# Ranks of tokens within an image pair: a scan over tiles on VectorE and three small products in place of eighteen wide ones

## Chip, cores and metric

The kernel runs on one core of one Trainium2 chip. The metric is the device time of one execution in microseconds. Three runs of the kernel before gave 541.8 us in the median (541.31 to 543.06).

PE is TensorE's matmul stream, PEld its weight loads, DVE is VectorE, ACT ScalarE, POOL GpSimd, SP SyncE.

## The reference, cut to what matters

```
x = x + conv_block(_ln_c(x))          # 16 images, 64 channels, 32x32; two binarized convolutions
t = _to_tokens(x)                     # 16384 tokens of 64
logits = _ln_t(t) @ gate_w + gate_b   # 16 experts
top_probs, top_idx = top_k(softmax(logits), 2)
hidden = silu(x @ w1[e]) * (x @ w2[e])
out = t + sum over the two chosen e of weight_e * (hidden @ w3[e])
```

Each token goes through two experts of sixteen, and gets their outputs with weights that sum to one.

## The kernel before, in words

**Routing by lines.** The sixteen experts are points of a 4 x 4 plane, and twenty lines of four points each cover every pair of points. A token is sent to the line that holds its two experts. Tokens of one line are gathered in pages of 128 tokens in DRAM, and a page is later multiplied with the four experts of its line. So each token needs a slot: the first row of its line's current page, plus its rank among the tokens of that line.

**Rounds.** The sixteen images are handled as eight pairs (q = 0 to 7). A pair is 2048 tokens: 128 partitions times TILES = 16 tiles. Each engine runs its own instruction list, written out by hand, in rounds t; in one round it works on up to five pairs at different stages: a = t (first normalization), s = t - 1 (the convolutions), b = t - 2 (second normalization, gate), r = t - 3 (choice of experts and line), z = t - 4 (slots, on DVE only). The order within a round is the order of the calls in the loops at L884 (PE), L650 (ACT) and L1520 (DVE). Semaphores join the engines.

**The steps around the change, for pair r or z.** PE's `count` (L865) gives for each token and line how many of the token's experts lie on the line. DVE's `find_line` (L1342) compares this with 1.5 and writes `line_hot`, a 0/1 array of 128 x 16 x 20. `find_line` is called between `newton_slack(0, a)` (L1246) and `newton_sum(0, a)` (L1252), two small steps of the reciprocal root `rstd` for pair a; for `rstd` wait ACT's `wide` (L576), then PE's `norm` (L831). PE's `rank` (L871 to L875) adds up in the PSUM tile `lines`: a product of `line_hot` with the strictly upper triangle (tokens of the same tile on partitions before), `left_b` (tokens left over from the pairs before, L872), and sixteen products with ones, one for each shift s in tiles, of (17 - s) x 20 columns, which add the tokens of all earlier tiles; tile 16 of the result is the total of each line. `rank` is the last call of PE's round; the first of the next is `variance(1, b)` (L819), which waits for ACT's `square2` (L602), and then the first convolution (L803). DVE's `slots(z)` (L1374 to L1414) turns ranks and totals into row numbers: twelve small steps over 20 lines, then four over 16 x 20, a reduction over lines, and a cast. Behind it stand `second_choice` (L1312 and on) with the three steps of the second root, whose second releases PE's `gate` (L848). POOL scatters the tokens of the pair to their slots (L498).

**The tail of the routing.** After pair 4 `order_pages` (L1431 to L1465) on DVE works out in which order pages are processed, PE turns it (L940), `order_rows` (L1470) casts it. SyncE waits for that before it loads pages (L392, L393). The roster of each page's experts (L1485 to L1507) and `rows_low` (L1513) stand on DVE ahead of `slots(7)`; the first expert products on PE (L971, L973) wait for both.

**The expert part**, from about 230 us of the profile on, handles 147 pages with PE, ACT and DVE in a pipeline, and scatters the results (L519). Nothing in it is touched.

## Time and profile before

| | us |
|---|---|
| median of 3 runs | 541.8 |
| lowest and highest run | 541.31, 543.06 |
| span of the profiled execution | 598.9 |
| busy in the profile: PE, PEld | 500.9, 436.7 |
| busy in the profile: DVE, ACT, POOL | 441.6, 396.0, 287.9 |

The profiled execution is longer than the runs that are timed. The page gives busy times and the chain of waits that ended last; a row of the timeline gives an instruction's start and length, and in brackets how long its engine sat idle before it and what ended that. "remote" in brackets, or "another core or an unknown queue" in the chain, is a wait whose end the profile ties to no instruction of this core. "x12" is twelve instructions merged in one row. Lengths of neighbouring rows may overlap, since the engines start an instruction before the one ahead has left.

### The profile page before, as it was taken

What the parts mean: (1) busy time and instruction counts of PE and PEld (TensorE: products, weight loads), DVE (VectorE), ACT (ScalarE), POOL (GpSimd) and SP (SyncE); (2) the same over time, 40 slices, a digit from 0 to 9 for tenths busy, and PEclk for the clock granted to TensorE, in tenths of its full rate; (3) what the DMA queues carried; (4) which work ended last, traced back from release to release, by engine and by line L of the source; (5) the groups of instructions that cost most, each with busy time, mean ns of one, the idle gap of its engine ahead of it and who ended that gap; (6) DMA issues with size and microseconds to landing.
All of it is one profiled execution on the core that took longest, in us unless ns stands there. A gap on an engine that the chain in (4) does not pass through costs nothing.

```text
span 598.9 us, 14226 instructions
## 1 busy us (share of the span) xinstructions
PE 500.9 (84%) x4186; PEld 436.7 (73%) x4186; DVE 441.6 (74%) x1242; ACT 396.0 (66%) x946; POOL 287.9 (48%) x378
## 2 busy tenths in 40 slices
PE   6899997896986627767889899999999999999854
PEld 5566665674764516757878799999998999899753
DVE  4567786685689697556676688888888888888653
ACT  5577885684765303456676588888787878778650
POOL 4000036666667675645555455454444544545351
PEclk9878997996979557879999899999999999999986
DMA  7941101011000012320122221232242425210404
GB/s 295 283 84 36 35 12 61 25 60 62 25 24 29 22 46 66 69 63 21 39 56 57 54 43 39 51 90 54 48 116 49 118 55 147 55 31 17 134 24 141
DMA packets 62664, 40.97 MB, mean 68 GB/s; under 512 B 50003, under 2 KB 54318, under 8 KB 62080
## 3 DMA queue, kind: packets, MB, share of 16 engines
q1 hardware_dynamic: 52208, 23.84, 17.5%
q0 software_dynamic: 8800, 8.94, 4.4%
q10 hardware_dynamic: 1584, 7.29, 3.2%
q8 instruction: 38, 0.62, 0.4%
q14 instruction: 34, 0.28, 0.2%
HBM read 21.46 MB, written 19.19 MB: 68 GB/s over the span
## 4 chain that ended last, share of the span: by engine, by line
PE 51%; DVE 17%; ACT 10%; issue 9%; another core or an unknown queue 6%; DMA 4%; SPq 3%; POOLq 0%; DVEq 0%; ACTq 0%; POOL 0%
PE up L971 9%; PE up L973 8%; PE turn L987 6%; PE up L803 5%; PE lines L1004 5%; PE small L819 3%; ACT xc L703 3%; DVE hidden L1589 2%; DMA x_in<-in_x 2%; PE lines L1006 2%; PE small L848 2%; PE up L789 2%; PE small L952 2%; PE up L778 2%
## 5 line engine op out<-in xcount | busy, mean ns | idle before, releaser
L519 POOL DMA_INDIRECT results<-result,page_in x147 | 154.3, 1050 | 152.0 <-ACT xc L703 103.5
L498 POOL DMA_INDIRECT pages<-payload,slot_int x128 | 127.6, 997 | 141.7 <-DVE slot_int L1414 73.5
L971 PE MATMUL up<-up_w,xs_hi 128*128 x588 | 163.5, 310 | 9.8 <-issue 5.1
L973 PE MATMUL up<-up_w,xs_lo 128*128 x588 | 150.0, 287 | 0.3 <-issue 0.3
L703 ACT ACTIVATE xc<-up 128x512 f32<-128x512 f32 x147 | 89.5, 609 | 76.5 <-PE up L973 48.4
L971 PEld LDWEIGHTS up<-up_w,xs_hi 128*128 128x128 f32 x588 | 114.1, 194 | 16.2 <-issue 13.7
L973 PEld LDWEIGHTS up<-up_w,xs_lo 128*128 128x128 f32 x588 | 114.7, 195 | 0.0
L1589 DVE SCALAR_TENSOR_TENSOR hidden<-up,page_in,xc 128x128 f32<-128x128 f32 x196 | 59.4, 344 | 43.2 <-ACT xc L703 35.4
L1599 DVE TENSOR_TENSOR hidden_lo<-turn,hidden_hi 128x512 f16<-128x512 f32 x98 | 67.0, 684 | 3.9 <-ACT hidden_hi L716 2.8
L987 PE MATMUL turn<-ident,hidden 128*128 128x128 f32 x392 | 60.7, 279 | 2.8 <-DVE branch L1599 1.6
L716 ACT ACTIVATE hidden_hi<-turn 128x512 f16<-128x512 f32 x98 | 60.9, 622 | 3.1 <-PE turn L987 2.5
L1004 PE MATMUL lines<-down_w,hidden_hi 128*128 x384 | 48.9, 221 | 12.7 <-DVE result L1616 9.6
L803 PE MATMUL up<-sign,conv_w 128*128 128x512 bf16 x192 | 50.1, 416 | 0.0
L987 PEld LDWEIGHTS turn<-ident,hidden 128*128 128x128 f32 x392 | 46.5, 143 | 3.6 <-issue 3.0
L1004 PEld LDWEIGHTS lines<-down_w,hidden_hi 128*128 128x128 f16 x384 | 36.0, 98 | 16.9 <-issue 15.8
L1006 PE MATMUL lines<-down_w,hidden_lo 128*128 x384 | 46.3, 194 | 1.5 <-issue 1.5
L707 ACT ACTIVATE branch<-up,page_in 128x128 f32<-128x128 f32 x146 | 46.8, 387 | 0.0
L707 ACT ACTIVATE sq<-up,page_in 128x128 f32<-128x128 f32 x148 | 46.6, 377 | 0.0
L1589 DVE SCALAR_TENSOR_TENSOR sq<-up,page_in,xc 128x128 f32<-128x128 f32 x98 | 29.6, 343 | 21.4 <-ACT xc L703 14.5
L819 PE MATMUL small<-mean_col,sq 128*128 128x2 f32 x256 | 32.2, 256 | 8.2 <-ACT sq L602 5.5
L819 PEld LDWEIGHTS small<-mean_col,sq 128*128 128x128 f32 x256 | 31.6, 200 | 9.4 <-ACT sq L602 6.3
L803 PEld LDWEIGHTS up<-sign,conv_w 128*128 128x128 bf16 x192 | 20.3, 111 | 23.5 <-issue 6.6
(262 smaller groups left out, 999.2 us busy)
## 6 DMA issues: line engine op xcount, KB each, us to landing
pages<-up_w ACTq DMA_DIRECT2D x4, 1332.0 KB, 9.9
page_in<-pages SPq DMA_DIRECT2D x147, 36.0 KB
page_in<-pages SPq DMA_DIRECT2D x147, 32.0 KB
x_in<-in_x SPq DMA_DIRECT2D x7, 512.0 KB
out<-up_raw SPq DMA_DIRECT2D x5, 512.0 KB, 4.8
results<-result,page_in POOLq DMA_INDIRECT x147
up_raw<-in_L_ffn_w SPq DMA_DIRECT2D x4, 512.0 KB, 16.8
pages<-payload,slot_int POOLq DMA_INDIRECT x128
```

Of the source, the lines that this page charges most:

```text
L498: pool.indirect_dma_start(out=pages, out_offset=bass.IndirectOffsetOnAxis(ap=slot_int[q % PAYLOADS][:, t:t + 1], axis=0), in_=payload[q % ...
L519: pool.indirect_dma_start(out=results, out_offset=bass.IndirectOffsetOnAxis(ap=page_in[g % LOADS][:, k, D + AT_TOKEN:D + AT_TOKEN + 1].bit ...
L703: act.activation(act_s[n % 2].rearrange("p (j h) -> p j h", j=PER_LINE), gates, ACT.Silu)\
L707: last = act.activation(scaled[n % 2][:, j * HID:(j + 1) * HID], up[n % 2][:, (2 * j + 1) * HID:(2 * j + 2) * HID], ACT.Copy, scale=page_i ...
L803: last = pe.matmul(cv[c], conv_w[:, which, t, :], image[:, c * ROWS + i:(c + 1) * ROWS + i, j:j + W], start=(t == 0), stop=(t == len(TAPS) ...
L819: last = pe.matmul(var_ps[n][:, 2 * j:2 * j + 2], sq[:, j * P:(j + 1) * P], mean_col[:, :], start=True, stop=True)
L971: pe.matmul(target, xs_hi[g % 2][:, k * P:(k + 1) * P], weights[:, bass.ds(e * 2, 2 * HID)], start=True, stop=False)
L973: last = pe.matmul(target, xs_lo[g % 2][:, k * P:(k + 1) * P], weights[:, bass.ds(e * 2, 2 * HID)], start=False, stop=True)
L987: last = pe.transpose(turn[n % 2][:, j * P:(j + 1) * P], hidden[n % 3][:, j * P:(j + 1) * P], ident[:, :])
L1004: pe.matmul(bank[:, at:at + 2 * D], hidden_hi[n % 3][:, j * P:(j + 1) * P], weights[:, bass.ds(e, 2 * D)], start=(j == 0), stop=False, ski ...
L1589: dve.scalar_tensor_tensor(out=hidden[n % 3][:, at], in0=values[:, j, :], scalar=page_in[g % LOADS][:, k, D + AT_WEIGHT + j:D + AT_WEIGHT ...
L1599: dve.tensor_tensor(hidden_lo[n % 3][:, :], turn[n % 2][:, :], hidden_hi[n % 3][:, :], ALU.subtract)\
```

## The change

`line_hot` is stored with lines outside and tiles inside. After the comparison DVE runs a scan along the 16 tiles of each line: `met` holds how many tokens of the partition, up to and with this tile, are on the line; `row_start` is 0 in the first tile of each line and 1 elsewhere, so that one scan over 320 elements starts anew for each line. `hot_ready`, for which PE waits, is signalled by the scan. PE's `rank` multiplies only the last tile of `met` (each partition's count) with the triangle and with ones, 20 columns each, and adds `left_b` to both, 40 columns. The ranks now count partition by partition and not tile by tile. In `slots` one step over 16 x 20 is added, which sums `met` - 1 and the partition's start; the steps after it read this sum from SBUF. Two reductions over lines read a strided view.

```diff
--- before.py
+++ after.py
@@ -171,9 +171,12 @@
         sided = sb("sided", [P, TILES, PER_LINE], F32)
         chosen_t = sb("chosen_t", [P, 2, P], BF16)
         by_y = sb("by_y", [P, TILES, PER_LINE], F32)
-        line_hot = sb("line_hot", [P, TILES + 1, LINES], BF16)
+        line_hot = sb("line_hot", [P, LINES, TILES], BF16)
+        met = sb("met", [P, LINES, TILES], BF16)
+        row_start = sb("row_start", [P, LINES, TILES], BF16)
         upright = sb("upright", [P, TILES], F32)
-        rank_old = sb("rank_old", [P, TILES, LINES], F32)
+        rank = sb("rank", [P, LINES, TILES], F32)
+        rank_old = sb("rank_old", [P, LINES, TILES], F32)
         slot = sb("slot", [P, TILES], F32)
         slot_int = [sb(f"slot_int{i}", [P, TILES], U32) for i in range(PAYLOADS)]
         payload = [sb(f"payload{i}", [P, TILES, ROW], F32) for i in range(PAYLOADS)]
@@ -252,7 +255,7 @@
         largest_ps = small[:, 32 + TILES * E:CW]
         chosen_ps = lines[:, (TILES + 1) * LINES:(TILES + 1) * LINES + P].bitcast(BF16)
         count_ps = lines[:, 0:TILES * LINES].rearrange("p (t l) -> p t l", l=LINES)
-        rank_ps = lines[:, 0:(TILES + 1) * LINES].rearrange("p (t l) -> p t l", l=LINES)
+        rank_ps = lines[:, 0:2 * LINES].rearrange("p (a l) -> p a l", l=LINES)
 
 
         table_link = sem("table_link")
@@ -868,12 +871,11 @@
 
             def rank(q):
                 pe.wait_ge(hot_ready, q + 1)
-                pe.matmul(rank_ps, upper_b[:, :], line_hot[:, :, :], start=True, stop=False, skip_group_check=True)
-                pe.matmul(rank_ps, ident_b[:, :], left_b[:, :].unsqueeze(1).to_broadcast([P, TILES + 1, LINES]),
-                          start=False, stop=False, skip_group_check=True)
-                for s in range(1, TILES + 1):
-                    last = pe.matmul(rank_ps[:, s:TILES + 1, :], ones_b[:, :], line_hot[:, 0:TILES + 1 - s, :],
-                                     start=False, stop=(s == TILES), skip_group_check=True)
+                in_row = met[:, :, TILES - 1]
+                pe.matmul(rank_ps[:, 0, :], upper_b[:, :], in_row, start=True, stop=False, skip_group_check=True)
+                pe.matmul(rank_ps[:, 1, :], ones_b[:, :], in_row, start=False, stop=False, skip_group_check=True)
+                last = pe.matmul(rank_ps, ident_b[:, :], left_b[:, :].unsqueeze(1).to_broadcast([P, 2, LINES]),
+                                 start=False, stop=True, skip_group_check=True)
                 last.then_inc(ranks_ready, 1)
 
 
@@ -1099,7 +1101,8 @@
                 dve.wait_ge(pool_made, PM_TABLES)
                 dve.tensor_copy(upper_b[:, :], upper[:, :])
                 dve.memset(ones_b[:, :], 1.0)
-                dve.memset(line_hot[:, TILES:TILES + 1, :], 0.0)
+                dve.memset(row_start[:, :, 0:1], 0.0)
+                dve.memset(row_start[:, :, 1:TILES], 1.0)
                 dve.memset(left_b[:, :], 0.0)
                 dve.memset(begun[0][:, :], 0.0)
                 dve.memset(begun_rows[0][:, :], 0.0)
@@ -1339,12 +1342,17 @@
                 dve.wait_ge(counts_ready, q + 1)
                 if q:
                     dve.wait_ge(ranks_ready, q)
-                dve.tensor_scalar(line_hot[:, 0:TILES, :], count_ps, 1.5, None, ALU.is_ge).then_inc(hot_ready, 1)
+                then(dve.tensor_scalar(line_hot[:, :, :].rearrange("p l t -> p t l"), count_ps, 1.5, None, ALU.is_ge))
+                settled()
+                dve.tensor_tensor_scan(out=met[:, :, :].rearrange("p l t -> p (l t)"),
+                                       data0=row_start[:, :, :].rearrange("p l t -> p (l t)"),
+                                       data1=line_hot[:, :, :].rearrange("p l t -> p (l t)"),
+                                       initial=0.0, op0=ALU.mult, op1=ALU.add).then_inc(hot_ready, 1)
 
             def line_parts(q):
                 rows = payload[q % PAYLOADS]
                 dve.wait_ge(hot_ready, q + 1)
-                then(dve.tensor_reduce(upright[:, :], line_hot[:, 0:TILES, 16:LINES], AX.X, ALU.max))
+                then(dve.tensor_reduce(upright[:, :], line_hot[:, 16:LINES, :].rearrange("p l t -> p t l"), AX.X, ALU.max))
                 settled()
                 then(dve.copy_predicated(by_x[:, :, :], spread(upright[:, :].bitcast(U32), PER_LINE), by_y[:, :, :]))
                 if q >= PAYLOADS:
@@ -1365,15 +1373,17 @@
 
             def slots(q):
                 def each(a):
-                    return a[:, :].unsqueeze(1).to_broadcast([P, TILES, LINES])
-                rank, total = rank_ps[:, 0:TILES, :], rank_ps[:, TILES, :]
+                    return a.unsqueeze(2).to_broadcast([P, LINES, TILES])
+                total = rank_ps[:, 1, :]
                 was, now = begun[q % 2], begun[(q + 1) % 2]
                 was_rows, now_rows = begun_rows[q % 2], begun_rows[(q + 1) % 2]
                 at = LINES * q
                 dve.wait_ge(ranks_ready, q + 1)
                 then(dve.tensor_scalar(rounded_up[:, :], total, (P - 1) / 2, ROUNDER, ALU.add, ALU.add))
                 then(dve.tensor_scalar(rounded[:, :], total, -(P - 1) / 2, ROUNDER, ALU.add, ALU.add))
-                settled(1)
+                then(dve.scalar_tensor_tensor(out=rank[:, :, :], in0=met[:, :, :], scalar=-1.0,
+                                              in1=each(rank_ps[:, 0, :]), op0=ALU.add, op1=ALU.add))
+                settled(2)
                 then(dve.scalar_tensor_tensor(out=added[:, :], in0=rounded_up[:, :], scalar=ROUNDER,
                                               in1=was_rows[:, :], op0=ALU.subtract, op1=ALU.subtract))
                 settled(1)
@@ -1394,20 +1404,20 @@
                 then(dve.tensor_tensor(back[:, :], back[:, :], was[:, :], ALU.mult))
                 then(dve.tensor_tensor(base_new[:, :], offset[:, :], full[:, :], ALU.add))
                 settled(1)
-                then(dve.scalar_tensor_tensor(out=rank_old[:, :, :], in0=rank, scalar=float(P), in1=each(back),
-                                              op0=ALU.is_lt, op1=ALU.mult))
+                then(dve.scalar_tensor_tensor(out=rank_old[:, :, :], in0=rank[:, :, :], scalar=float(P),
+                                              in1=each(back[:, :]), op0=ALU.is_lt, op1=ALU.mult))
                 then(dve.scalar_tensor_tensor(out=base_old[:, :], in0=total, scalar=float(P), in1=back[:, :],
                                               op0=ALU.is_lt, op1=ALU.mult))
                 settled(1)
-                then(dve.tensor_tensor(rank_old[:, :, :], rank_old[:, :, :], rank, ALU.add))
+                then(dve.tensor_tensor(rank_old[:, :, :], rank_old[:, :, :], rank[:, :, :], ALU.add))
                 settled(1)
                 then(dve.tensor_tensor(base[:, :], base_old[:, :], base_new[:, :], ALU.add))
                 settled(1)
-                then(dve.tensor_tensor(rank_old[:, :, :], rank_old[:, :, :], each(offset), ALU.add))
-                settled()
-                then(dve.tensor_tensor(rank_old[:, :, :], rank_old[:, :, :], line_hot[:, 0:TILES, :], ALU.mult))
-                settled()
-                then(dve.tensor_reduce(slot[:, :], rank_old[:, :, :], AX.X, ALU.add))
+                then(dve.tensor_tensor(rank_old[:, :, :], rank_old[:, :, :], each(offset[:, :]), ALU.add))
+                settled()
+                then(dve.tensor_tensor(rank_old[:, :, :], rank_old[:, :, :], line_hot[:, :, :], ALU.mult))
+                settled()
+                then(dve.tensor_reduce(slot[:, :], rank_old[:, :, :].rearrange("p l t -> p t l"), AX.X, ALU.add))
                 if q >= PAYLOADS:
                     dve.wait_ge(scattered[q % PAYLOADS], 16 * TILES * (q // PAYLOADS))
                 settled()
```

## Rows read from the trace of the kernel before

**Rows 1.** The page: the shares of the chain that ended last, by engine.

```profile
PE 51%; DVE 17%; ACT 10%; issue 9%; another core or an unknown queue 6%; DMA 4%; SPq 3%; POOLq 0%; DVEq 0%; ACTq 0%; POOL 0%
```

**Rows 2.** Groups by line and shape: out<-in, shapes, count, busy us, mean ns, idle before.

```profile
L1589 DVE SCALAR_TENSOR_TENSOR hidden<-up,page_in,xc 128x128 f32<-128x128 f32 x196 | 59.4, 344 | 43.2 <-ACT xc L703 35.4 <-issue 4.6 <-PE turn L987 3.1
...
L1397 DVE SCALAR_TENSOR_TENSOR rank_old<-lines,back 128x320 f32<-128x320 f32 x8 | 3.9, 491 | 0.0
...
L1342 DVE TENSOR_SCALAR line_hot<-lines 128x320 bf16<-128x320 f32 x8 | 3.9, 484 | 0.7 <-PE lines L865 0.6
...
L875 PE MATMUL lines<-line_hot,ones_b 128*128 128x320 bf16 x8 | 3.1, 392 | 0.0
...
L1383 DVE TENSOR_TENSOR_SCAN opened<-all_one,opened,added 128x20 f32<-128x20 f32 x8 | 2.1, 260 | 0.0
...
L875 PE MATMUL lines<-line_hot,ones_b 128*128 128x20 bf16 x8 | 1.4, 174 | 0.0
...
L1399 DVE SCALAR_TENSOR_TENSOR base_old<-lines,back 128x20 f32<-128x20 f32 x8 | 1.3, 168 | 0.0
```

**Rows 3.** Chain of waits in order of time, 66 to 178 us: start, us, what.

```profile
71.41 0.40 DVE line_hot L1342
...
102.54 1.78 PE small L819 x16
...
125.01 1.78 PE small L819 x16
...
151.10 1.78 PE small L819 x16
```

**Rows 4.** Timeline of PE, 72 to 147 us: start, us, line, operation, idle time before it.

```profile
72.82 1.17 PE L831 MATMUL turn<-ident,rstd_wide 128*128 128x128 f32 x8 [0.91 <-ACT rstd_wide L576]
...
77.73 1.95 PE L819 MATMUL small<-mean_col,sq 128*128 128x2 f32 x16 [1.40 <-ACT sq L602]
...
145.66 1.97 PE L831 MATMUL turn<-ident,rstd_wide 128*128 128x128 f32 x8 [1.22 <-ACT rstd_wide L576]
```

**Rows 5.** Timeline of ACT: the second square of rounds 4, 5 and 6.

```profile
100.07 0.60 ACT L602 ACTIVATE sq<-up 128x512 f32<-128x512 f32 x1 [1.23 <-issue]
...
123.58 0.60 ACT L602 ACTIVATE sq<-up 128x512 f32<-128x512 f32 x1 [0.36 <-issue]
...
149.37 0.60 ACT L602 ACTIVATE sq<-up 128x512 f32<-128x512 f32 x1 [1.23 <-PE up L789]
```

**Rows 6.** PE timeline, opening convolutions; then windows: PE, PEld, DVE, ACT, POOL busy, PEclk, DMA.

```profile
36.51 4.45 PE L803 MATMUL up<-sign,conv_w 128*128 128x512 bf16 x12
...
126.65 2.81 PE L803 MATMUL up<-sign,conv_w 128*128 128x512 bf16 x12
...
78.00:82.00 4.00, 4.00 (x27) 2.64 (x28) 3.90 (x21) 3.33 (x7) 0.00 (x0) 1.00 0.01 2
...
57.70:61.30 3.60, 3.60 (x11) 1.26 (x10) 3.43 (x13) 2.96 (x6) 0.00 (x0) 0.53 0.00 0
```

**Rows 7.** Timeline of all engines, 126 to 132 us: DVE's slots and PE's gate.

```profile
126.85 0.18 DVE L1374 TENSOR_SCALAR rounded_up<-lines 128x20 f32<-128x20 f32 x1 [0.43 <-remote]
...
131.99 1.86 PEld L848 LDWEIGHTS small<-gate_mat,xc 128*128 128x128 f32 x16 [0.34 <-DVE slack L1252]
```

**Rows 8.** Timeline of DVE from slots(4) to the first expert page.

```profile
175.46 0.18 DVE L1374 TENSOR_SCALAR rounded_up<-lines 128x20 f32<-128x20 f32 x1 [0.37 <-PE lines L875]
...
178.45 0.49 DVE L1408 TENSOR_TENSOR rank_old<-rank_old,line_hot 128x320 f32<-128x320 f32 x1
178.98 0.49 DVE L1410 TENSOR_REDUCE slot<-rank_old 128x16 f32<-128x320 f32 x1
...
216.20 0.27 DVE L1470 CAST order<-small 2x128 int32<-2x128 f32 x1
...
229.71 0.69 DVE L1513 TENSOR_TENSOR xs_lo<-small,xs_hi 128x512 fp32r<-128x512 f32 x1 [0.69 <-ACT xs_hi L696]
...
234.44 0.61 DVE L1589 SCALAR_TENSOR_TENSOR hidden<-up,page_in,xc 128x128 f32<-128x128 f32 x2
```

## The prediction

> **What bounds the kernel now.** I read the page first, and in it the chain of waits [rows 1]. The chain lies mostly on PE, and one step in twenty is "another core or an unknown queue". On one core there is no other core: these are pauses in which several engines stop together, and most of them should belong to the profiled execution. Its span is 598.9 us, the median of the runs is 541.8 us, so 57 us of it are not in an ordinary run. I make the sum against the profile's own times, carry the difference over in absolute us to 541.8, and say below where a pause colours a term.
>
> Then I read the list of groups by line for what is removed and added [rows 2], the chain of waits in order of time between 66 and 178 us [rows 3], and the timelines of PE, ACT and DVE around the rank products [rows 4 to 6]. The pairs run through rounds t (one about every 20 to 25 us). The path in one round is: variance(0) on PE, logarithm and exponential on ACT, newton_slack, find_line, newton_sum and newton_root on DVE, wide on ACT, norm on PE, center2(1), rank, variance(1), the next convolution. Two things are to be seen. find_line stands between two small steps of the root, so its 0.40 us are on the path [rows 3], and PE really idles for that root: 0.91 us in round 3, in which no pause lies, 1.22 us in round 6 [rows 4]. And rank stands between center2(1) and variance(1), which also needs ACT's second square [rows 5]. After 178 us there is no image left to convolve but the last; DVE is busy nearly without a gap, and the chain runs mostly on it up to the cast of the page order at 216.20 us, on which SyncE's page loads wait [rows 8].
>
> **What goes from PE.** Per pair 16 wide products of 392 down to 174 ns each [rows 2], which overlap, and two of 340 columns. In its place come three products of 20, 20 and 40 columns; the narrowest of the old ones took 174 ns, so the three end in about 0.3 us. What this gives is not the block but the distance from the end of the second square to the start of variance(1) [rows 3, 5]: in round 4 102.54 - (100.07 + 0.60) = 1.87, in round 5 125.01 - (123.58 + 0.60) = 0.83, in round 6 151.10 - (149.37 + 0.60) = 1.13. In round 3 it is nothing: PE waits 1.40 us for ACT's square, which is behind a weight copy [rows 4]. In round 7 the block holds up DVE's slots by 0.37 us [rows 8]; from then on the ranks are ready long before they are read.
>
> **What comes to DVE, in find_line.** The comparison stays (0.48 us, now with a strided output; a row of the other side, the strided reduction, costs nothing extra, so I count none). It must now be settled, which two dependent steps show as 0.04 us (0.49 long, started 0.53 apart, at 178.45 and 178.98 [rows 8]), and the scan over 320 elements follows. The only scan in the trace is of 20 elements and takes 260 ns, where a one-pass operation of 20 takes 168 and one of 320 takes 491, a slope of 1.08 ns an element [rows 2]. So the scan has 92 ns too much. Part of it is the start value that it reads by pointer: an operation of 128 elements with a pointer scalar takes 344 ns where the slope gives 284, so 60 ns. The 32 left over 20 elements are 1.6 ns an element, somewhat over one more pass. The new scan has a constant start: 0.49 + 0.35 = 0.84 us with one more pass, 0.49 + 0.51 = 1.0 with 1.6 ns; I take 0.9. The bounds are 0.49 (no second pass, all 92 ns fixed) and 0.49 + 320 x 4.6 ns = 1.96 us (all 92 ns by element). The next operation begins some 0.08 us before the end of the one ahead (0.48 long, 0.40 of the chain). So find_line grows from 0.40 to 0.48 + 0.04 + 0.9 - 0.08 = 1.34 us: d = 0.94, with bounds 0.53 and 2.0.
>
> The Trainium skill (DVE: opcode table, instruction layouts, handler registers and perf-mode slots, section Datapath and trigger behaviour) says that the built-in scan runs at half throughput. The rows agree with it within 0.2 us; by it alone the scan would be 0.84 us and the sum below 0.5 us smaller. This is a rule that speaks against moving the work here.
>
> Queued behind find_line on DVE are newton_sum and newton_root; for them wait wide on ACT, norm and everything after it on PE, and x_norm.
>
> **In slots.** One operation of 320 elements is added, 0.49 us long, of which 0.40 count before the next begins; it reads the small PSUM result once, the later steps read SBUF, the later steps read SBUF in place of PSUM, and their price I leave as it is.. Behind it stand the whole chain of slots and second_choice, whose newton steps release PE's gate. The four steps in another layout, the reductions over strided views and the changed memsets at the start are edits with one answer: nothing, since they have the same element count or stand where DVE idles.
>
> **The sum, rounds 3 to 7** (the sign + is slower). Round 3: +0.94. Round 4: 0.94 - 1.87 = -0.93; part of this gain comes from the clock at its low level after a pause, at the full clock it is nearer to 1.1. Round 5: 0.94 - 0.83 = +0.11. But then DVE comes late: it idled 0.43 us before slots, and the gate after it waited for DVE already [rows 7]; DVE's shift is 0.94 + 0.40 - 0.43 = 0.91 and replaces the 0.11, so +0.80 more. Round 6: 0.94 - 1.13 = -0.19. Round 7: 0.94 - 0.37 = +0.57. Together +1.3.
>
> **The tail** (from 176 us to the first expert pages). DVE is the path: slots of pairs 4 to 7 bring 4 x 0.40 = 1.6, find_line of pairs 5 to 7 brings 3 x 0.94 = 2.8. Only one gap absorbs some: 0.69 us before the low halves of the first rows [rows 8], because the first turned rows come earlier when the last rank block no longer stands ahead of them on PE. The first expert blocks then wait for DVE: the first hidden step is queued behind slots and comes at 234.44 [rows 8]. Tail +3.7. Later everything shifts by this: the expert part is paced by PE, ACT and DVE with the same work as before.
>
> Without the clock: +5.0, and 8 more for each us by which d is larger.
>
> **The clock.** The convolution that opens a round took 4.45 us for its 12 products in rounds 2 and 3, which no rank block precedes, and 2.81 in all five rounds that one precedes [rows 6]; the granted clock was 0.53 in the first case and 1.00 in the second, that is 1.2 GHz for much of the stretch against 2.4. What PE did before differs: in the slow cases idle time, norm, center2 and then variance, with products of two columns; in the fast ones the dense rank block as well. Without it, rounds 4 to 8 look to PE like 2 and 3, with more idle time still (d). One cold convolution costs 4.45 - 2.81 = 1.64 us on the path. That none of five turns cold or all five are the ends; the places where the clock changes drift against the rounds, so I take two, +3.3. The Trainium skill (TensorE: Matmul & The Clock Gate, section What's actually happening) says that the throttled level is the default and activity lifts it, which by itself would make it all five, +8.2.
>
> Forecast: 541.8 + 5.0 + 3.3 = 550.1.
>
> **Rivals.**
> (1) Faster: PE sets the rounds and DVE's additions are hidden. In an ordinary run without pauses ACT and DVE might be early enough. For it: PE holds half of the chain [rows 1]. Against it: PE's wait for the root in the round without a pause [rows 4]. Its place is norm's wait: if rstd comes before center2(0) has ended, d costs nothing; that decides from 0.9 us of slack on. Then rounds 4 to 7 give 1.87 + 0.83 + 1.13 + 0.37 = 4.2, and with the tail hidden in the page loads the time is 537.6.
> (2) It cancels: d is hidden in the rounds, the tail costs its 3.7: 541.8 - 4.2 + 3.7 = 541.3.
> (3) All five convolutions turn cold: 541.8 + 5.0 + 8.2 = 555.0. For it: two of two without a rank block.
> (4) The scan costs 1.96 us, or strided 2-byte writes cost as much: 541.8 + 5.0 + 8 x 1.06 = 555.3, with cold convolutions up to 559.
> (5) The change does not do what it says, for instance if three dependent small products with strided input last as long as the block. The 20-column product took 174 ns, so three can't; I give it nothing of its own.
>
> **Chances.** Forecast, with none to three cold convolutions, 0.51, its own range 546 to 552. Rival 1: 0.13. Rival 2: 0.11. Rival 3: 0.13. Rival 4: 0.12. The range must leave out no more than 0.2: it goes from 541 (rival 2 in, rival 1 out) to 556 (rivals 3 and 4 in, with 0.05 beyond). A measurement of this kernel can tell some 0.3%, 1.6 us, from no change: faster 0.13, same 0.11, slower 0.76.
>
> **What would show it.** In the profile of the changed kernel: the scan over 320 elements with mean 0.84 to 1.0 us; PE's idle time before norm in a round without a pause near 0.91 + 0.94 us; the rank products under 0.4 us a pair and variance(1) starting when the square ends; the cast of the order and the first expert product later relative to the last residual by some 2 and 3 us; the granted clock at 0.5 in some of the convolutions that follow a rank. It would be wrong if norm doesn't wait for rstd, if DVE has gaps of more than a us between 176 and 230 us, or if the scan's mean lies outside 0.5 to 2.0 us.

## The result and the profile after

The changed kernel took 563.5 us in the median of four runs (561.7 to 564.0), against 541.6 of the kernel before: a ratio of 1.039, 95% interval 1.036 to 1.043. It is slower by 21.9 us, as forecast in sign, but well outside the range of 541 to 556. One run of the experiments below, 552.7 us of read_moved, was in a slower state and is left out of its median and range.

The page of the profile after, the lines that answer to [rows 1] and to the busy times of the table (busy us and share of the span; then the shares of the chain by engine):

```profile
span 562.2 us, 14003 instructions
...
PE 480.6 (85%) x4066; PEld 418.3 (74%) x4066; DVE 459.0 (82%) x1259; ACT 395.9 (70%) x946; POOL 289.8 (52%) x378
...
PE 50%; DVE 30%; ACT 7%; issue 7%; DMA 3%; SPq 1%; POOL 1%; POOLq 0%; DVEq 0%; ACTq 0%
```

This profile has hardly a pause: its span is 562.2 us beside a median of 563.5. The one of before had 57 us of them. So I took the kernel before once more, and compare with that profile from here on; its page:

```profile
span 538.8 us, 14226 instructions
...
PE 478.5 (89%) x4186; PEld 421.4 (78%) x4186; DVE 438.7 (81%) x1242; ACT 394.3 (73%) x946; POOL 287.1 (53%) x378
...
PE 55%; DVE 27%; ACT 7%; issue 7%; DMA 2%; POOL 1%; ACTq 0%; POOLq 0%; SPq 0%; DVEq 0%
```

PE's busy time is nearly the same in both (480.6 and 478.5 us), although the wide products are gone. DVE's grew by 20 us; its share of the chain rose from 27 to 30%, and PE's fell from 55 to 50%.

The groups by line of after that answer to [rows 2] (out<-in, shapes, count, busy us, mean ns, idle before):

```profile
L1345 DVE TENSOR_SCALAR line_hot<-lines 128x320 bf16<-128x320 f32 x8 | 11.9, 1494 | 0.6 <-PE lines L868 0.6
...
L1347 DVE TENSOR_TENSOR_SCAN met<-row_start,line_hot 128x320 bf16<-128x320 bf16 x8 | 6.6, 824 | 0.3
L1420 DVE TENSOR_REDUCE slot<-rank_old 128x16 f32<-128x320 f32 x8 | 5.5, 692 | 0.3
...
L875 PE MATMUL lines<-met,upper_b 128*128 128x20 bf16 x8 | 1.7, 214 | 6.0 <-DVE met L1347 6.0
```

The scan is 0.824 us. The comparison, which I had left at 0.48 us, takes 1.49. The reduction over the turned array takes 0.69 in place of 0.49. The first of the small products takes 0.21 us.

The chain of waits (start, us, what) over one round of the second profile of before, round 5:

```profile
109.03 0.48 DVE line_hot L1342
...
114.43 1.18 PE lines L875 x16
115.61 1.78 PE small L819 x16
117.39 2.67 PE up L803 x12
```

And of after, round 4:

```profile
95.90 1.50 DVE line_hot L1345
...
97.43 0.82 DVE met L1347
...
102.91 0.61 ACT sq L605
...
105.50 4.31 PE up L806 x12
```

(The chain and the timeline differ by some 0.15 us in where they put the end of a product.) find_line stands in the chain with 1.50 and 0.82 us, the rank block is gone from it, ACT's square stands in its place, and the opening convolution takes 4.31 us. The timeline of PE for the same round of after:

```profile
99.24 1.92 PE L834 MATMUL turn<-ident,rstd_wide 128*128 128x128 f32 x8 [2.76 <-ACT rstd_wide L579]
...
103.56 1.95 PE L822 MATMUL small<-mean_col,sq 128*128 128x2 f32 x16 [0.60 <-ACT sq L605]
105.36 4.45 PE L806 MATMUL up<-sign,conv_w 128*128 128x512 bf16 x12
```

PE idles 2.76 us before norm, in place of 0.91 in [rows 4] and in all five rounds of the second profile: 1.85 us more. That is what find_line has grown by: from its start to the last step of the root, on DVE, it was 0.60 us (90.11 to 90.71 in the second profile of before) and is 2.45 us (95.90 to 98.35 in after). The granted clock, from the windows between the first and the sixth find_line (PE, PEld, DVE, ACT, POOL busy, PEclk, DMA), of before and of after:

```profile
69.62:169.34 99.72, 91.74 (x607) 69.60 (x606) 83.42 (x276) 79.14 (x164) 67.63 (x68) 0.95 0.14 47
```

```profile
71.91:185.41 113.50, 94.44 (x532) 67.61 (x531) 95.87 (x286) 79.77 (x164) 71.09 (x70) 0.86 0.13 42
```

The rows of each from DVE's timeline in the tail answer to [rows 8]: the cast of the order, the low halves and the first hidden step.

```profile
193.62 0.27 DVE L1470 CAST order<-small 2x128 int32<-2x128 f32 x1
...
207.08 0.69 DVE L1513 TENSOR_TENSOR xs_lo<-small,xs_hi 128x512 fp32r<-128x512 f32 x1 [0.77 <-ACT xs_hi L696]
...
211.81 0.60 DVE L1589 SCALAR_TENSOR_TENSOR hidden<-up,page_in,xc 128x128 f32<-128x128 f32 x2
```

```profile
214.11 0.27 DVE L1480 CAST order<-small 2x128 int32<-2x128 f32 x1
...
229.22 0.68 DVE L1523 TENSOR_TENSOR xs_lo<-small,xs_hi 128x512 fp32r<-128x512 f32 x1
...
234.52 0.60 DVE L1599 SCALAR_TENSOR_TENSOR hidden<-up,page_in,xc 128x128 f32<-128x128 f32 x2
```

The 0.77 us for which DVE waited before the low halves are gone; DVE has no such gap there now. Everything from the first hidden step on takes as long as before (538.8 - 211.8 = 327.0 us, 562.2 - 234.5 = 327.7).

### The profile page after: what moved, and what is told of

It is laid out like the page before. It is cut to its first block, busy times and chain, and to the rows that moved or that the text cites. A ratio compares the mean times of both kernels' runs of the same rounds, so it can differ in the third digit from the quotient of the medians.

```text
span 562.2 us, 14003 instructions
## 1 busy us (share of the span) xinstructions
PE 480.6 (85%) x4066; PEld 418.3 (74%) x4066; DVE 459.0 (82%) x1259; ACT 395.9 (70%) x946; POOL 289.8 (52%) x378
## 4 chain that ended last, share of the span: by engine, by line
PE 50%; DVE 30%; ACT 7%; issue 7%; DMA 3%; SPq 1%; POOL 1%; POOLq 0%; DVEq 0%; ACTq 0%
PE up L806 9%; PE up L973 8%; PE up L975 6%; PE small L822 5%; DVE hidden L1599 4%; PE lines L1006 4%; DVE xs_lo L1523 4%; ACT xc L706 4%; PE turn L989 3%; DVE hidden L1604 3%; PE small L851 3%; PE small L954 3%; DMA x_in<-in_x 3%; PE up L781 2%; DVE line_hot L1345 2%
## 5 line engine op out<-in xcount | busy, mean ns | idle before, releaser
L522 POOL DMA_INDIRECT results<-result,page_in x147 | 152.7, 1039 | 128.6 <-ACT xc L706 106.4
L501 POOL DMA_INDIRECT pages<-payload,slot_int x128 | 131.1, 1024 | 126.3 <-DVE slot_int L1424 82.0
L973 PE MATMUL up<-up_w,xs_hi 128*128 x588 | 161.0, 306 | 4.5 <-DVE xs_lo L1523 3.6
L975 PE MATMUL up<-up_w,xs_lo 128*128 x588 | 147.5, 283 | 0.0
L973 PEld LDWEIGHTS up<-up_w,xs_hi 128*128 128x128 f32 x588 | 112.5, 191 | 8.8 <-issue 5.7
L975 PEld LDWEIGHTS up<-up_w,xs_lo 128*128 128x128 f32 x588 | 112.9, 192 | 0.0
L989 PE MATMUL turn<-ident,hidden 128*128 128x128 f32 x392 | 59.3, 274 | 0.8 <-DVE up_raw L1633 0.7
L806 PE MATMUL up<-sign,conv_w 128*128 128x512 bf16 x192 | 56.9, 458 | 0.0
L806 PEld LDWEIGHTS up<-sign,conv_w 128*128 128x128 bf16 x192 | 21.8, 119 | 27.9 <-issue 15.0
```

The source lines that it names most:

```text
L501: pool.indirect_dma_start(out=pages, out_offset=bass.IndirectOffsetOnAxis(ap=slot_int[q % PAYLOADS][:, t:t + 1], axis=0), in_=payload[q % ...
L522: pool.indirect_dma_start(out=results, out_offset=bass.IndirectOffsetOnAxis(ap=page_in[g % LOADS][:, k, D + AT_TOKEN:D + AT_TOKEN + 1].bit ...
L806: last = pe.matmul(cv[c], conv_w[:, which, t, :], image[:, c * ROWS + i:(c + 1) * ROWS + i, j:j + W], start=(t == 0), stop=(t == len(TAPS) ...
L973: pe.matmul(target, xs_hi[g % 2][:, k * P:(k + 1) * P], weights[:, bass.ds(e * 2, 2 * HID)], start=True, stop=False)
L975: last = pe.matmul(target, xs_lo[g % 2][:, k * P:(k + 1) * P], weights[:, bass.ds(e * 2, 2 * HID)], start=False, stop=True)
L989: last = pe.transpose(turn[n % 2][:, j * P:(j + 1) * P], hidden[n % 3][:, j * P:(j + 1) * P], ident[:, :])
```

## The experiments

This table has one profile of each kernel: PE's idle time before norm (in idle_filler and gaps what the added products leave of it), the lengths of the five opening convolutions that follow a rank, the time from the first find_line to the sixth (rounds 3 to 8), from the sixth to the cast of the order, the granted clock in the five rounds, and the median of the runs (of before, again there is one run, 540.5 us; the kernel before had 541.6 beside after and between 540.9 and 542.2 beside the others).

| kernel | idle | opening convolutions | five rounds | to the cast | clock | median |
|---|---|---|---|---|---|---|
| before, again | 0.91 | 2.8 2.8 2.8 2.8 2.8 | 99.7 | 24.3 | 0.95 | 540.5 |
| before_scans | 2.46 | 2.8 2.8 2.8 2.8 2.8 | 111.6 | 27.6 | 0.88 | 559.8 |
| before_moved | 0.63 | 5.0 2.8 2.8 2.8 2.8 | 99.3 | 24.4 | 0.93 | 541.7 |
| after | 2.76 | 4.5 4.5 2.8 4.5 4.1 | 113.5 | 28.7 | 0.86 | 563.5 |
| read_strided | 1.75 | 4.4 5.3 4.9 4.3 5.3 | 113.7 | 26.8 | 0.83 | 558.2 |
| dense | 2.76 | 2.8 2.8 2.8 2.8 2.8 | 113.2 | 28.7 | 0.88 | 564.8 |
| idle_filler | 1.70 | 4.2 2.8 4.5 2.8 2.8 | 112.8 | 28.7 | 0.94 | 560.6 |
| read_moved | 0.63 | 4.2 4.5 4.5 4.2 4.5 | 101.1 | 26.9 | 0.88 | 547.6 |
| slots_moved | 0.63 | 4.2 4.5 4.5 4.1 4.5 | 101.3 | 27.3 | 0.88 | 547.7 |
| gap_late | 0.63 | 5.3 2.8 2.8 2.8 4.4 | 102.2 | 27.2 | 0.92 | 549.1 |
| gaps | 0.20 | 5.0 4.3 2.8 4.5 4.2 | 105.5 | 27.2 | 0.89 | 549.5 |

One thing is to be known for reading it: the medians scatter. The kernel before lay between 538.5 and 545.8 us in 17 runs, read_moved between 542.2 and 549.1 in 9. Differences below some 3 us between two kernels with four runs each are not told apart here.

The five rounds can be divided further at the starts of PE's steps, each column summed over the five rounds: find_line to norm; norm to variance(1), with center2 and the rank products between; variance(1) to the opening convolution; the convolution; from its end to the gate; from the gate to the next find_line.

| kernel | to norm | to variance | to convolution | convolution | to gate | to find_line |
|---|---|---|---|---|---|---|
| before, again | 7.45 | 23.07 | 8.96 | 13.20 | 11.87 | 35.17 |
| before_scans | 15.25 | 27.67 | 8.95 | 13.20 | 11.38 | 35.17 |
| before_moved | 4.00 | 21.17 | 9.99 | 15.45 | 11.87 | 36.87 |
| after | 16.70 | 21.45 | 9.03 | 19.46 | 11.68 | 35.18 |
| read_strided | 11.67 | 18.31 | 13.70 | 23.26 | 11.69 | 35.06 |
| dense | 16.69 | 27.23 | 8.93 | 13.22 | 11.92 | 35.25 |
| idle_filler | 16.79 | 16.98 | 10.67 | 16.22 | 15.10 | 37.03 |
| read_moved | 3.97 | 18.13 | 9.26 | 20.90 | 11.88 | 36.92 |
| slots_moved | 3.99 | 18.13 | 9.28 | 20.84 | 12.18 | 36.85 |
| gap_late | 3.99 | 19.26 | 9.88 | 17.20 | 14.71 | 37.16 |

Two theories stood against each other. A: what find_line costs on DVE is on the path of the root and of the tail. B: most of the loss is PE's clock, since the rank block that held it up is gone.

**before_again.** The kernel before, unchanged.

> The kernel before once more, for a profile with fewer pauses. If the pauses of the first profile belong to the profiling, the span is near 541 us; PE's idle time before norm is near 0.9 us in every round with a rank block, and the five opening convolutions that follow a rank block take 2.81 us. If the ratio to the changed kernel hides in the expert part, this profile shows its first expert product as late as that of the changed kernel.

Span 538.8 us, idle time before norm 0.91 us in all five rounds, all five opening convolutions 2.8 us. So the pauses belonged to the first profile, and the expert part is not where the loss lies.

**read_strided.**

```diff
-dve.tensor_scalar(line_hot[:, :, :].rearrange("p l t -> p t l"), count_ps, 1.5, None, ALU.is_ge)
+dve.tensor_scalar(line_hot[:, :, :], count_ps.rearrange("p t l -> p l t"), 1.5, None, ALU.is_ge)
```

> The changed kernel, but the comparison reads the counts from PSUM in turned order and writes line_hot densely. Theory A (what find_line costs on DVE is on the path of the root and of the tail): the comparison falls from 1.49 to about 0.5 us and the time falls by eight times 1.0, from 563.5 to 555.5. Theory B (most of the loss is the convolutions at the low clock): four slow ones stay and the time falls by 2 us at most. If reading in turned order is as dear as writing, nothing changes.

558.2 us (ratio to before 1.027, 1.022 to 1.033): 5.3 us faster than after, between the 8 of theory A and the 2 at most of B. The group by line:

```profile
L1345 DVE TENSOR_SCALAR line_hot<-lines 128x320 bf16<-128x320 f32 x8 | 3.9, 483 | 0.6 <-PE lines L868 0.6
```

Reading PSUM in turned order costs nothing (483 ns, as in the kernel before), and the idle time before norm fell by the whole 1.01 us in each round. In the tail the time fell by 1.9 us up to the cast and by 0.9 us from there to the first hidden step, as A says (two and one find_line). The rest of the 4.7 us between the two spans lies ahead of the first find_line (0.8) and behind the first hidden step (1.3), where nothing was changed. But the five rounds did not get shorter (113.7 us against 113.5): all five opening convolutions were now slow, some to 5.3 us. By the second table the way to norm gave back 5.0 us and that to variance 3.1, and the convolution with the products of two columns ahead of it took 8.5. What DVE gave back in the rounds, the clock took in this profile.

**dense.**

```diff
                 in_row = met[:, :, TILES - 1]
+                for _ in range(12):
+                    pe.matmul(lines[:, 40:320], ones_b[:, :], line_hot[:, :, :].rearrange("p l t -> p (l t)")[:, 0:280],
+                              start=True, stop=True, skip_group_check=True)
```

> The changed kernel with twelve further products of 280 columns ahead of the three of each rank, into columns nobody reads: as many columns as the eighteen had, and no change on VectorE. Theory B: the opening convolutions after a rank all take 2.8 us again, four times 1.5 us come back, less what the extra products hold up variance: 3 to 6 us faster than the changed kernel. Theory A alone: no convolution matters, 563.5 us or some us more.

564.8 us (1.043, 1.039 to 1.047), not faster than after at all. And yet the convolutions did what B says, all five at 2.8 us. PE's timeline of round 4:

```profile
97.04 1.97 PE L834 MATMUL turn<-ident,rstd_wide 128*128 128x128 f32 x8 [2.76 <-ACT rstd_wide L579]
98.80 1.91 PE L792 MATMUL up<-x,center_mat 128*128 128x256 f32 x4
100.51 2.45 PE L876 MATMUL lines<-line_hot,ones_b 128*128 128x280 bf16 x12
...
104.69 2.80 PE L806 MATMUL up<-sign,conv_w 128*128 128x512 bf16 x12
```

Norm, center2 and the added products now lie in the slow stretch, which follows the long idle time, and the 2.45 us of the products stand on the path in place of the slow convolution. Over the five rounds 5.8 us more pass from norm to variance and 6.2 less in the convolution. So work before a convolution changes the clock of the convolution, but the slow stretch is not avoided by it; it is paid elsewhere.

**before_scans.** The other way round, the cost on DVE alone, with the rank block kept:

```diff
-                dve.tensor_scalar(line_hot[:, 0:TILES, :], count_ps, 1.5, None, ALU.is_ge).then_inc(hot_ready, 1)
+                then(dve.tensor_scalar(line_hot[:, 0:TILES, :], count_ps, 1.5, None, ALU.is_ge))
+                settled()
+                then(dve.tensor_tensor_scan(out=met[:, :, :].rearrange("p t l -> p (t l)"),
...
+                dve.tensor_tensor_scan(out=met2[:, :, :].rearrange("p t l -> p (t l)"),
...
+                                       initial=0.0, op0=ALU.mult, op1=ALU.add).then_inc(hot_ready, 1)
```

> The kernel before with two scans of 320 elements added to find_line, whose results nobody reads; the eighteen products stay. find_line grows by about 0.04 + 0.74 + 0.82 = 1.6 us. Theory A (a us in find_line is a us on the path, in all eight rounds): PE idles 0.91 + 1.6 us before norm, and the time is 541.6 + 8 x 1.6 = 554.4. Theory B (the rank block keeps the convolution at the full clock): no slow convolution after a rank. If only the idle time before norm sets the clock, convolutions turn slow here too and the time is near 560.

559.8 us (1.031, 1.025 to 1.037): above the 554.4 of A alone and at the 560 named for the case that idle time alone sets the clock, but by another way than that one said. No opening convolution is slow. PE's timeline of a round:

```profile
96.66 1.97 PE L834 MATMUL turn<-ident,rstd_wide 128*128 128x128 f32 x8 [2.46 <-ACT rstd_wide L579]
98.42 1.91 PE L792 MATMUL up<-x,center_mat 128*128 128x256 f32 x4
...
100.69 2.13 PE L878 MATMUL lines<-line_hot,ones_b 128*128 128x320 bf16 x16
...
104.47 2.80 PE L806 MATMUL up<-sign,conv_w 128*128 128x512 bf16 x12
```

The slow stretch lies on norm, center2 and the rank block (1.97, 1.91 and 2.13 us; at the full clock 1.18, 1.03 and 1.34). The five rounds grew by 11.9 us, of which 5 x 1.55 = 7.8 are idle time and 4.1 the clock. That it is the clock shows in PE's busy time: the same 607 products took 97.69 us in the five rounds, in place of 91.74. In after the rounds grew by 13.8, of which 5 x 1.85 = 9.3 are idle time and 4.5 the rest. So with nothing changed on PE a wait on DVE of 1.55 us costs 18 us, where the change, with 1.85 us, costs 22, the clock's share included. This is what decides between the theories: A holds, and most of the loss needs no missing block.

**idle_filler.**

```diff
+                if r >= 0 and a < PAIRS:
+                    pe.wait_ge(channels_ready[0], a - 1)
+                    for _ in range(5):
+                        pe.matmul(turn[0][:, :], ones_b[:, :],
+                                  conv_w[:, :, :, :].rearrange("p a b c -> p (a b c)")[:, 0:CW], start=True, stop=True)
                 if a < PAIRS:
                     for c in range(CH):
                         norm(c, a)
```

> The changed kernel with five products of 512 columns on PE in the 2.76 us for which it idles before norm (rounds 3 to 7), into a PSUM tile that norm overwrites. They last 1.1 to 2.2 us, less than the idle time, so they cost nothing by themselves. Theory B, if PE's work before the convolution sets its clock: norm, center2 and the opening convolutions run at the full clock, 4 to 8 us faster than the changed kernel, 556 to 559. If only what lies close before the convolution counts, the slow convolutions stay and the time is that of the changed kernel.

560.6 us (1.034, 1.028 to 1.040), some 3 us below after, less than expected and at the edge of what can be told. The granted clock rose from 0.86 to 0.94, norm ran at the full clock in all five rounds, three convolutions of five were fast. But the five rounds lasted 112.8 us, hardly less. The second table says where it went: 4.5 us came back between norm and variance and 3.2 in the convolutions, and 1.6 were lost ahead of them, 3.4 on the way to the gate and 1.9 behind it. In the three rounds in which norm, center2 and the convolution were all fast (4, 6 and 7), PE then idled 0.46, 0.51 and 2.37 us before the gate, for DVE's second root; the second profile of before has such a wait in round 7 only, 0.43 us. PE's work in the gap lifts the clock; it doesn't shorten what DVE has to do.

**slots_moved and read_moved.** Both read PSUM in turned order and have find_line behind the root:

```diff
-                if 0 <= r < PAIRS:
-                    find_line(r)
                 if a < PAIRS:
                     newton_sum(0, a)
                     newton_root(0, a)
                 if 0 <= r < PAIRS:
+                    find_line(r)
                     line_parts(r)
```

slots_moved also computes slots in the old order, with a dense last reduction, reading met and line_hot turned.

> The changed kernel with three repairs: the comparison writes densely and reads PSUM in turned order, slots works in the old order (its last reduction is dense) and reads met and line_hot turned, and find_line stands behind the two steps of the root. Theory A: the writing gives 8 us, the order some 5 x 1.3 us of rounds 3 to 7, the reduction about 1 us: 563.5 - 15 = 548 or so, above the kernel before because the tail and the slow convolutions remain. Rival: if what is lost is PE's clock, it stays above 555.

> The changed kernel with the turned reading of the counts and find_line behind the two steps of the root, slots as in the changed kernel. It tells the two differences of the run slots_moved from the run read_strided (558.2 to 547.7 us) apart. Theory: all of it is the order, since the turned reading of line_hot in slots costs about what its dense reduction gives; so 547 to 549 us. Rival: half of it is slots; then 552 to 554.

547.7 us (1.012, 1.004 to 1.020) and 547.6 us (1.008, 1.005 to 1.012), as expected by theory A. The order by itself is worth some 10 us: the five rounds fell from 113.7 (read_strided) to 101.1 us. More than the 1.12 us of idle time each (5.6 us) is in that. PE's busy time in the rounds fell by 5.8 us for as many products but two (97.33 to 91.52), which is the clock again. The order within slots is worth nothing; its reduction is back at 0.49 us, but the turned reading of 2-byte line_hot has made another step dearer (0.49 before):

```profile
L1418 DVE TENSOR_TENSOR rank_old<-rank_old,line_hot 128x320 f32<-128x320 f32 x8 | 6.0, 746 | 0.3
```

PE's timeline of round 5 of slots_moved:

```profile
110.76 1.18 PE L834 MATMUL turn<-ident,rstd_wide 128*128 128x128 f32 x8 [0.63 <-ACT rstd_wide L579]
...
113.77 1.95 PE L822 MATMUL small<-mean_col,sq 128*128 128x2 f32 x16 [0.88 <-ACT sq L605]
115.58 4.45 PE L806 MATMUL up<-sign,conv_w 128*128 128x512 bf16 x12
```

Norm is at the full clock, its idle time is 0.63 us, less than in the kernel before. PE now idles 0.88 us for ACT's square, and all five convolutions are slow. A round lasts 19.98 us, where the kernel before needs 18.9 in its best and 20.5 in its other rounds. The eighteen products are saved, and 1.65 us come back as a slow convolution. That is not the only thing that holds the round: DVE releases the gate of this round at most 0.5 us before PE comes to it (its second root ends 12.0 us after find_line begins, the gate begins 12.5 us after). In before_moved DVE was ready at 10.9 us; with the scan and the added step of slots in it, this way is 1.2 us longer. And most of the 6 us by which both kernels lie above before_moved is in the tail: from the sixth find_line to the first hidden step 46.4 us in read_moved and 47.3 in slots_moved, 42.5 in before_moved.

**before_moved.** The same reordering alone, in the kernel before.

> The kernel before with find_line behind the two steps of the root, nothing else. Theory A: its 0.40 us leave the path in rounds 3 to 7, 2 us faster, 539.6. Rival: the first step of the root takes its place as a wait for the step ahead (a semaphore of 0.1 us), so less than 1.5 us.

541.7 us, ratio 1.000 (0.997 to 1.004): nothing. The idle time fell from 0.91 to 0.63 us only, since the second step of the root now waits for the first to settle, which find_line had covered: the two begin 0.21 us apart (92.88, 93.09). Five times 0.28 are 1.4 us, and the scatter hides them.

**gap_late and gaps.** slots_moved with work in PE's gaps: the loop of dense with range(5) (gap_late), and with it that of idle_filler with range(2) (gaps).

> The run slots_moved with five products of 280 columns (0.6 us at the full clock) ahead of each rank, where PE idles 0.6 to 0.9 us for the second square. Theory B: PE's work just before variance decides the clock of the opening convolution; more of the five take 2.8 us, each giving 1.6 us, while the products cost little: 541 to 546. Rival: too little work to hold the clock; all five stay slow and the time is 547.7 to 551.

> The run gap_late with two further products of 512 columns in PE's 0.63 us of idle time before norm, into the tile that norm overwrites. If work in both gaps holds the clock as the rank block did, all opening convolutions take 2.8 us and norm its short 1.2 us: 538 to 542, level with the kernel before or 1 to 3 us below it. If not, it is as gap_late.

549.1 us (1.013, 1.008 to 1.019) and 549.5 us (1.012, 1.008 to 1.016). Neither came near 541. PE's timeline of gap_late, round 5 and then round 6:

```profile
115.88 1.97 PE L834 MATMUL turn<-ident,rstd_wide 128*128 128x128 f32 x8 [0.63 <-ACT rstd_wide L579]
117.64 1.84 PE L792 MATMUL up<-x,center_mat 128*128 128x256 f32 x4
...
121.98 2.80 PE L806 MATMUL up<-sign,conv_w 128*128 128x512 bf16 x12
...
135.85 1.17 PE L834 MATMUL turn<-ident,rstd_wide 128*128 128x128 f32 x8 [0.64 <-ACT rstd_wide L579]
...
140.68 2.81 PE L806 MATMUL up<-sign,conv_w 128*128 128x512 bf16 x12
...
147.10 1.97 PE L851 MATMUL small<-gate_mat,xc 128*128 128x32 f32 x16 [1.02 <-DVE slack L1258]
```

In round 5 the convolution is fast, norm and center2 are slow, and the round is as long as in slots_moved, 19.96 us. It is the picture of dense once more: the slow stretch moved. In round 6 norm and the convolution are both fast, and now PE idles 1.02 us before the gate, for DVE's second root. The round lasts 19.62 us; the rounds of before_moved with both fast lasted 18.65. So behind the clock stands a second limit, DVE's way from find_line through slots to the second root; it takes some 1.0 us of what a fast round could give. And the tail of both runs, 47.2 us from the sixth find_line to the first hidden step, is 4.7 us longer than in before_moved, which the clock in the rounds doesn't touch. gaps had fewer fast convolutions than gap_late, and I have no reason for that which the runs show.

**probes.** After the last addition, fourteen single operations of 320 elements, three times over, with the same lengths within 0.02 us each time.

> The changed kernel with fourteen VectorE operations of 320 elements after the last addition, three times over, each alone: comparison and addition with dense and turned output of 2 and 4 bytes, turned reading from PSUM, reductions over dense and turned input. Theory: writing 2-byte elements 32 bytes apart is what makes 1.49 us out of 0.49, and 4-byte elements written 64 bytes apart, or reading in turned order, cost 0.5. Rival: any order with such a step costs three times as much, whichever the size and the side. The time is some 25 us above that of the changed kernel by the added operations.

Timeline of DVE. In order: comparison SBUF to SBUF, 2 bytes out, dense, then 32 bytes apart; 4 bytes out, dense, then 64 bytes apart; comparison from PSUM to 2 bytes, read dense, then turned; addition of two SBUF arrays to 2 bytes, 32 bytes apart, then dense; reduction of 4-byte elements, dense, then 64 bytes apart.

```profile
558.44 0.32 DVE L1667 TENSOR_SCALAR met<-rank_old 128x320 bf16<-128x320 f32 x1
558.79 0.83 DVE L1669 TENSOR_SCALAR met<-rank_old 128x320 bf16<-128x320 f32 x1
...
560.94 0.33 DVE L1675 TENSOR_SCALAR rank<-rank_old 128x320 f32<-128x320 f32 x1
561.30 0.43 DVE L1677 TENSOR_SCALAR rank<-rank_old 128x320 f32<-128x320 f32 x1
561.77 0.49 DVE L1679 TENSOR_SCALAR row_start<-lines 128x320 bf16<-128x320 f32 x1
562.29 0.49 DVE L1681 TENSOR_SCALAR row_start<-lines 128x320 bf16<-128x320 f32 x1
562.82 1.50 DVE L1683 TENSOR_TENSOR met<-rank_old,rank 128x320 bf16<-128x320 f32 x1
564.35 0.49 DVE L1685 TENSOR_TENSOR met<-rank_old,rank 128x320 bf16<-128x320 f32 x1
564.88 0.48 DVE L1687 TENSOR_REDUCE slot<-rank_old 128x16 f32<-128x320 f32 x1
565.40 0.69 DVE L1689 TENSOR_REDUCE slot<-rank_old 128x16 f32<-128x320 f32 x1
```

The 2-byte elements written 32 bytes apart take 0.83 where the dense ones take 0.32, and 1.50 where they take 0.49. At 4 bytes 64 bytes apart costs 0.10, reading SBUF turned 0.20, reading PSUM turned nothing. So not any step costs three times as much, as the rival had it, and writing 2-byte elements is the dear case, as the theory said. But the theory is right only in part: it had turned reading at no cost, and turned reading from SBUF costs 0.20 to 0.25 us here and in slots_moved. Nor is the size told apart from the step: no operation wrote 2-byte elements 64 bytes apart or 4-byte ones 32 bytes apart. And a comparison with one input from SBUF lost 0.51 us by it, the other two forms 1.01; why stays open. The Trainium skill (Advanced Engine Details and Errata, section SBUF Cachelines) says that SBUF has lines of 16 bytes, that accesses which each meet another line are penalized, and that what stride is tolerated depends on the type. The direction agrees; that 4-byte writes with twice the stride cost so little, and 2-byte writes three times the dense ones, the page doesn't say.

## Why the prediction was wrong

**What held.** The place of the cost: find_line stands between two steps of the root, PE waits for the root, and each us in find_line is a us of idle time on PE (0.91 + 1.85 = 2.76, 0.91 + 0.84 = 1.75, 0.91 + 1.55 = 2.46; DVE's timeline shows the same growths). The scan: 0.824 us, a little under the 0.84 of one more pass, where I had taken 0.9. The tail: with a find_line that is 0.84 us longer (read_strided) the stretch to the cast grew by 2.5 us, where the forecast's terms give 2 x 0.84 and twice the added step of slots, 0.8. That opening convolutions turn slow without the block before them: four of five in after, all five in read_moved.

**The step that failed** is the half-sentence in the part on find_line that the strided output "costs nothing extra, so I count none". It costs 1.01 us per pair (1.494 against 0.483). The change writes 2-byte elements 32 bytes apart, and I took the price from a reduction, which reads. In the kernel before, the reduction that fills by_y reads 8 bytes apart and takes 0.41 us, as its dense neighbour by_x does; that says nothing of writing, and not even reading stays free at a wider step: the last reduction of slots, which reads 64 bytes apart in after, costs 0.20 us more (0.69 against 0.49). With the writing, d is 1.85 in place of 0.94, and by the forecast's own rule of 8 us per us the sum without the clock is 5.0 + 8 x 0.91 = 12.3 in place of 5.0.

I had the writing in rival 4, with a chance of 0.12, and its d of 2.0 was large enough for the 1.85. But it stands there at 555.3, and up to 559 with two slow convolutions, while four of five were slow. Dear writing and the slow convolutions of rival 3 came together, and the range, which ends at 556, held each of them only alone. I gave the scan a bound on either side and the writing a zero in the sum; a term without a row wants such bounds too.

**The terms of the five rounds.** The second table has them for before_again and after.

| us | forecast | measured |
|---|---|---|
| wait for the root | 5 x 0.94 = 4.7 | 9.3 |
| gate waits for DVE (round 5) | 0.8 | -0.2 |
| saved on PE between norm and variance | -4.2 | -1.6 |
| slow opening convolutions | 3.3 | 6.3 |
| sum | 4.6 | 13.8 |

The saving on PE came from a profile with pauses: the sixteen products of round 4 took 2.15 us in it, and 1.34 in the second profile. In the second the distance from the end of the square to variance is 95.11 - 94.57 = 0.54 in round 4 and 115.61 - 114.78 = 0.83 in round 5, so about 3 for the four rounds; less than that was saved, since norm and center2 were in part slower in after. The gate of round 5 came later in after because PE came later: DVE was ready 0.2 us ahead of it (14.20 and 14.39 us after find_line began), and the gate shows no wait. The wait that the forecast counted there appears where PE is faster, as in gap_late. The clock: I counted two slow convolutions, 3.3 us; this profile has four, with 6.3 us.

**By stretches**, from the two profiles without pauses: 2.3 us lie ahead of the first changed step (the first find_line begins at 69.62 and at 71.91 us; among all eleven profiles of the table between 68.1 and 71.9, so it is within the scatter between profiles); 13.8 in the five rounds; 4.4 up to the cast; 2.2 from there to the first hidden step; 0.7 behind it. The sum is the 23.4 us between the spans. The forecast had 4.6 for the rounds with the clock, and 3.7 for the tail, where 4.4 + 2.2 = 6.6 were measured; with 3 x 0.91 = 2.7 for the writing the forecast's 3.7 is 6.4.

**Of the clock the forecast had half the cause.** It made the missing rank block the reason. That the block matters is shown by read_moved beside before_moved, with the same idle time of 0.63 us before norm: without the block the granted clock is 0.88 in place of 0.93 and all five opening convolutions are slow in place of one. That it isn't needed is shown by before_scans: with the block in place and only the wait on DVE longer, the clock falls from 0.95 to 0.88 and the way from norm to variance takes 4.6 us more. Nor did the block's return help: dense, with as many columns, is no faster than after. So on the path the block's saving is more than given back: read_moved saves 3.0 us on the way to variance and 0.7 behind it against before_moved, and pays 5.5 in the convolutions. What exactly brings the clock down stays open, and each of these sums is of one profile. That lifting it (0.86 to 0.94) hardly shortened the rounds has one reason in the traces: when PE is fast, the gate waits for DVE.

## What to carry to other kernels

Before an operation is put on an engine, ask for what that engine is holding up where it is put: ahead of the root's steps each us of find_line was a us of idle time on PE before norm, behind them none (558.2 against 547.6 us for the same work). Behind them it still counts on DVE's way to the gate and in the tail. A turned view is free or not by where it is read or written: here turned reading from PSUM cost nothing, turned reading from SBUF some 0.2 us, and writing 2-byte elements 32 bytes apart into SBUF 1.0 us for 320 of them. And a saving on PE is to be taken from rounds without pauses, and counted only after asking whether the clock keeps what it had and which engine ends next when PE comes earlier.

## What the runs showed of the hardware

- A scan of 320 2-byte elements takes 0.824 us, a one-pass operation of as many with two inputs 0.49: 1.04 ns an element more, about one more pass.
- On DVE 2-byte elements written 32 bytes apart: 1.50 us for 320 in place of 0.49, from PSUM or for two inputs; 0.83 in place of 0.32 for a comparison from SBUF. 4-byte elements written 64 bytes apart: 0.43 in place of 0.33. 2-byte elements written 4 bytes apart by the same comparison: 0.35. Reductions that read SBUF 64 bytes apart: 0.69 in place of 0.48; a multiplication that read its 2-byte input turned 0.75 in place of 0.49. A comparison that read PSUM 80 bytes apart: no difference.
- Twelve bf16 products of 512 columns took 2.81 us at the full clock, and 4.1 to 5.3 us where the slow level fell on them. The fastest and the slowest of the nine runs of read_moved, 542.2 and 549.1 us, had mean granted clocks of 0.919 and 0.908.
- Pauses of the first profile, in which several engines stopped together, added 60 us to its span (598.9 against 538.8 us). Over the five rounds its granted clock was 0.88, in the second profile 0.95.
